# First layer norm: the inverse deviation over four columns, turned and spread by TensorE

## The chip, the cores and the metric

One core of a Trainium2 chip runs the whole computation in one launch. Its engines work side by side, each through its own queue in order, and meet by semaphores: TensorE (PE), VectorE (DVE), ScalarE (ACT), GpSimd (POOL), and SyncE (SP), which here only issues transfers. The metric is the device time of one execution in microseconds.

## The reference

The inputs are `x` (16 x 64 x 2048) and a context `ctx_4096` (16 x 1601 x 2048). Three blocks add to `x` in turn, each behind a layer norm:

```python
x = x + _L0_xattn_ref(_layernorm(x, axis=-1), ctx_4096, conv_w, bn_gamma, bn_beta)
x = x + _L0_attn_ref(_layernorm(x, axis=-1), wq, wk, wv, wo)
x = x + _L0_ffn_ref(_layernorm(x, axis=-1), gate_w, base_w, base_b, lora_A, lora_B)

def _layernorm(x, axis=-1, eps=1e-05):
    m = jnp.mean(x, axis=axis, keepdims=True)
    v = jnp.var(x, axis=axis, keepdims=True)
    return (x - m) / jnp.sqrt(v + eps)
```

The first block ranks, for each of the 16 batches and 2048 positions, the 1601 rows of the context, marks which of the 64 channels of `x` belong to the 38 highest of all, takes maximum and mean over the marked and the other channels, runs a short convolution with batch norm and sigmoid over them, and weights the channels. The second is causal attention with rotary positions (32 heads, 8 of keys and values), the third a linear layer with eight low-rank experts of which two are chosen.

The change is in the first layer norm: for each of the 16 x 64 = 1024 rows of `x` (a batch and a channel) a mean, a variance and 1 / sqrt(variance + eps) over 2048 positions.

## The kernel before, in words

**Layout.** `x` lies in SBUF as `XN`, 128 partitions x 2 halves x 16 steps x 512 columns. A column is one of the 1024 rows of `x` (8 batches x 64 channels a half), and its 2048 positions lie over 128 partitions x 16 steps. So a sum over positions is a product of a 128x128 matrix of ones with each of the 16 steps, added up in PSUM: each partition of the result then holds the same 512 sums. The mean and the inverse deviation of a half are therefore 128 x 512 tiles in which all 128 partitions are equal.

**The search around it.** The first 680 us rank the context. 256 tiles of 128 x 1601 values (16 batches x 16 steps) stream through a ring of 14 buffers; SP issues tile n when tile n - 14 has been used (`search_sync`, L426). A round `i` handles four tiles, in 66 rounds. DVE takes the eight largest of the 64 channels of each (L580) and bounds from them (L585), and writes, for each tile, two masks of what is larger than a bound, `b` and `c` (L440, one buffer of three after the other). ACT counts what is above another bound with a sign activation and its accumulator (`sign_scalar`, L642). PE adds up each mask, 13 products (`count_tensor`, L693), and ACT sums the result into a count (`counts_scalar`, L650). The counts decide the bounds of the next masks (L593, L601, L613, L617). POOL copies the 64 channels aside (L681).

**The layer norm inside it.** Its instructions are put into the queues between those of the search, at fixed rounds, by `LN0_SUM`, `LN0_MEAN`, `LN0_SUB` and `LN0_VAR`, each with a round for half 0 and one for half 1. In `search_vector` `ln0_vector` comes behind the fifth mask of a round (`k == 4`); in `search_scalar` `ln0_scalar` comes behind the fourth sign and the count of slot 1; in `search_tensor` `ln0_tensor` is called with `u` = 0 behind the second mask, with `u` = 1 behind the fourth, and so on. PE sums `XN` (L549), ACT scales to the mean (L531), DVE subtracts it in pairs of steps, every second round (L514), ACT squares one step a round into `lsq` (L539), and PE sums the squares (L556). Squares of half 1 run in rounds 41 to 56, so while half 0 gets its deviation in rounds 43 and 44. For half 0 (PSUM bank `ps[7]`, result tile `Rs`) and half 1 (`ps[6]`, result tile `Mn`) the deviation is made over the full 128 x 512: DVE multiplies by 1/L and adds eps (L520), ACT takes the root (L542), and a round later DVE the reciprocal (L523). When all masks are issued (`masked` reaches NMASKS) POOL multiplies `XN` by the result (`ln0_out_gpsimd`, L710), and the later stages begin.

## Time and profile before

| | us |
|---|---|
| median of 3 runs | 2283.42 |
| the three runs | 2282.82, 2283.42, 2288.04 |
| profiled execution | 2279.7 |
| its span | 2277.9 |
| DVE busy | 1402.7 (62%) |
| PE busy | 2004.4 (88%) |
| ACT busy | 1013.3 (44%) |
| POOL busy | 1021.4 (45%) |

The span is the time between the first and the last record of the profiled execution; its own time has some 1.8 us around it. The shares are means over stages with different limits: the search takes the first 680 us, then come the rest of the first block and, from about 860 us on, the products of attention and of the linear layer, in which PE is full. A row with a line number names the line of the kernel; where two numbers follow an arrow in brackets, the engine stood idle so long before the instruction, and what is named released it. Two records of one engine can overlap by some 0.1 us, so what an instruction costs its queue is read from its start to the start of the next one.

### The profile page before, as it was taken

The numbers are of one execution on the slowest core, as the hardware profiler recorded it, in microseconds if no ns is written. First come the engines' busy times: TensorE is split into PE (matmuls) and PEld (weight loads), VectorE is DVE, ScalarE is ACT, GpSimd is POOL, SyncE is SP. The second block draws the span as 40 slices with busy tenths as digits, with TensorE's granted clock in tenths as the row PEclk, the third lists the DMA queues.
The fourth block names the chain that finished last, engine by engine and source line by source line (L and its number), as shares of the span: only waits on it lengthen the run. The fifth ranks groups of instructions, "written<-read, shape, count | busy, mean of one in ns | idle before, by whom it ended". The sixth has DMA issues, their size and how long they took to land. (4 is left out here: it accounts for less than half of the span.)

```text
span 2277.9 us, 39061 instructions
## 1 busy us (share of the span) xinstructions
PE 2004.4 (88%) x15226; PEld 1633.7 (72%) x15226; DVE 1402.7 (62%) x2179; ACT 1013.3 (44%) x2014; POOL 1021.4 (45%) x930
## 2 busy tenths in 40 slices
PE   4778788777764947999999999999999999999999
PEld 3666566555554836787877888878778878888887
DVE  6999999999999989844444531144445425731111
ACT  7778788877840355423222422223223322422221
POOL 1223332222226522755564456556555445644554
PEclk9999999999987869999999999999999999999999
DMA  9999999889930114632225443322244345434443
GB/s 382 375 355 378 337 323 322 318 293 319 333 145 15 75 43 132 185 107 75 80 97 181 139 145 109 94 83 77 83 161 144 126 136 213 131 129 125 140 139 117
DMA packets 158392, 407.69 MB, mean 179 GB/s; under 512 B 15616, under 2 KB 44544, under 8 KB 156544
## 3 DMA queue, kind: packets, MB, share of 16 engines
q1 hardware_dynamic: 157920, 403.55, 51.7%
q8 instruction: 121, 1.98, 0.3%
q0 software_dynamic: 288, 1.64, 0.2%
q14 instruction: 63, 0.52, 0.1%
HBM read 379.96 MB, written 25.17 MB: 178 GB/s over the span
## 5 line engine op out<-in xcount | busy, mean ns | idle before, releaser
L1238 POOL TENSOR_TENSOR t<-t,t 128x512 fp32r<-128x512 f32 (+1 forms) x488 | 652.5, 1348 | 658.7 <-ACT t L1231 585.5
L1789 PE MATMUL ps<-t,t 128*128 128x512 f32 x1856 | 737.6, 397 | 12.4 <-POOL t L1238 7.1
L1791 PE MATMUL ps<-t,t 128*128 128x512 f32 x1856 | 723.8, 390 | 0.0
L1790 PE MATMUL ps<-t,t 128*128 128x512 f32 x1856 | 723.1, 390 | 0.0
L693 PE MATMUL ps<-t,t 128*128 128x128 bf16 (+1 forms) x6656 | 450.1, 221 | 181.3 <-DVE t L440 163.3
L1231 ACT ACTIVATE t<-t 128x512 fp32r<-128x512 f32 (+1 forms) x488 | 296.2, 608 | 696.1 <-PE ps L1791 381.6
L693 PEld LDWEIGHTS ps<-t,t 128*128 128x128 bf16 x6656 | 386.4, 100 | 279.8 <-DVE t L440 248.0
L440 DVE TENSOR_SCALAR t<-t,t 128x1601 bf16<-128x1601 f32 x512 | 516.2, 1050 | 4.6 <-DVE t L601 0.9
L642 ACT ACTIVATE t<-t,t 128x1601 bf16<-128x1601 f32 x256 | 416.9, 1628 | 62.7 <-DVE t L585 59.0
L1789 PEld LDWEIGHTS ps<-t,t 128*128 128x128 f32 x1856 | 348.3, 188 | 92.7 <-POOL t L1238 11.6
L1791 PEld LDWEIGHTS ps<-t,t 128*128 128x128 f32 x1856 | 348.3, 188 | 74.1
L1790 PEld LDWEIGHTS ps<-t,t 128*128 128x128 f32 x1856 | 348.7, 188 | 71.1 <-issue 1.4
L681 POOL COPY t<-t 128x64 f32<-128x64 f32 x256 | 163.2, 638 | 376.2 <-DMA t<-ctxT 375.9
L1749 DVE TENSOR_TENSOR t<-ps,t 128x512 f32<-128x512 f32 x32 | 22.1, 689 | 232.9 <-PE ps L1791 232.8
L1324 DVE SCALAR_TENSOR_TENSOR t<-ps,t 128x512 f32<-128x512 f32 x32 | 22.1, 691 | 177.0 <-PE ps L1316 177.0
L1746 DVE TENSOR_TENSOR t<-ps,t 128x512 f32<-128x512 f32 x32 | 22.1, 691 | 169.6 <-PE ps L1791 169.6
L650 ACT ACTIVATE t<-ps 128x128 bf16<-128x128 f32 x260 | 68.5, 263 | 92.8 <-PE ps L693 92.4
L1480 DVE TENSOR_REDUCE t<-t 128x128 f32<-128x2048 f32 x24 | 91.7, 3856 | 12.4 <-ACT t L1508 9.7
L1338 ACT ACTIVATE t<-t 128x512 f32<-128x512 f32 x32 | 20.2, 632 | 152.0 <-DVE t L1328 152.0
L562 PE MATMUL ps<-t,t 128*128 128x128 f32 x256 | 56.8, 398 | 29.7 <-POOL t L710 29.7
L562 PEld LDWEIGHTS ps<-t,t 128*128 128x128 f32 x256 | 53.5, 228 | 32.9 <-POOL t L710 30.3
L1271 POOL TENSOR_TENSOR t<-t,t 128x512 f32<-128x512 f32 x40 | 52.6, 1314 | 37.3 <-DVE t L1262 37.1
(210 smaller groups left out, 1692.9 us busy)
## 6 DMA issues: line engine op xcount, KB each, us to landing
t<-ctxT SPq DMA_DIRECT2D x256, 800.5 KB, 6.4
t<-wqkv SPq DMA_DIRECT2D x192, 256.0 KB, 3.1
t<-wo SPq DMA_DIRECT2D x128, 256.0 KB, 4.5
t<-wb SPq DMA_DIRECT2D x128, 256.0 KB, 3.5
t<-xT SPq DMA_DIRECT2D x48, 256.0 KB, 6.7
t<-x1d SPq DMA_DIRECT2D x32, 256.0 KB, 4.8
x2d<-t SPq DMA_DIRECT2D x32, 256.0 KB, 2.0
t<-x2d SPq DMA_DIRECT2D x8, 1024.0 KB, 7.4
```

The costliest lines, as they stand in the source:

```text
L440: e.tensor_scalar(Mb[k % 3][:, :], ring[n % NR][:, :], bound, None, ALU.is_gt).then_inc(masked, 1)
L562: return e.matmul(dst, ident, src, start=(c == 0), stop=(c == C - 1))
L642: e.activation(scr[:, :], ring[n % NR][:, :], ACT.Sign, bias=nT[:, n:n + 1], scale=SHRINK, accum_out=cntA[:, n:n + 1]).then_inc(signed, 1)
L650: e.activation(jr[:, :], ps[k % 6][:, 0:128], ACT.Copy, accum_out=sums[:, k:k + 1]).then_inc(counts_out, 1)
L681: e.tensor_copy(cand[b % 2][:, t, :], ring[n % NR][:, 0:C]).then_inc(cand_copied, 1)
L693: m = e.matmul(ps[s % 6][:, 0:w], (identh if kind == "b" else identb)[:, :], Mb[k % 3][:, 128 * c:128 * c + w], start=(first and c == 0), ...
L1231: e.activation(wh[r][:, 0:nk, :], raw[r][:, 0:nk, :], ACT.Copy).then_inc(w_hi, 1)
L1238: e.tensor_tensor(wlo[r][:, 0:nk, :], raw[r][:, 0:nk, :], wh[r][:, 0:nk, :].bitcast(F32), ALU.subtract).then_inc(w_lo, 1)
L1480: e.tensor_reduce(R1[:, cs], over_t((x if step == "s" else sq)[:, :, cs]), AX.X, ALU.add).then_inc(l_sum, 1)
L1789: e.matmul(bank[:, :], wh[r][:, q, :], xl, start=(kt == 0), stop=False)
L1790: e.matmul(bank[:, :], wlo[r][:, q, :], xh, start=False, stop=False)
L1791: m = e.matmul(bank[:, :], wh[r][:, q, :], xh, start=False, stop=(c == NCH[p] - 1 and q == nk - 1))
```

## The change

The deviation is the same in all 128 partitions of a 128 x 512 tile. The new code works it out once per column of a 128 x 4 tile, where the 512 values of a half lie over 128 partitions x 4 columns, and takes these steps (h is the half, `LN0_VAR` is now 43 and 58):

- round LN0_VAR: ACT copies the sums of squares from PSUM to SBUF (L545, semaphore `ln0_flat`)
- the round behind it: PE multiplies each of the four 128-column blocks of this copy, as weights, with one column of the identity, which lays the 512 sums over partitions, in four columns of PSUM (L573, `ln0_turned`); DVE scales and adds eps on 128 x 4 (L521); ACT takes the root in place (L548)
- the next: DVE takes the reciprocal of 128 x 4 (L524); ACT makes four copies of the 128 x 128 identity, scaled by partition with one of the four columns (L552), which is a row of diagonal blocks
- the next: PE multiplies a matrix of ones with them (L577), which spreads the 512 values over all partitions, and ACT copies the result to SBUF (L555, `ln0_rstd`)

```diff
-    LN0_SUM, LN0_MEAN, LN0_SUB, LN0_VAR = (15, 30), (23, 39), (24, 40), (43, 59)
+    LN0_SUM, LN0_MEAN, LN0_SUB, LN0_VAR = (15, 30), (23, 39), (24, 40), (43, 58)
...
+    ln0_inv = [sc[:, 40 + 4 * h:44 + 4 * h] for h in range(2)]
...
     def ln0_vector(e, i):
...
-            if i == LN0_VAR[h]:
-                e.wait_ge(ln0_sqsum, 16 * h + 16)
-                if h:
-                    e.wait_ge(ln0_sub, 16)
-                e.tensor_scalar(ln0_rs[h][:, :], ln0_sums[h][:, :], 1.0 / L, EPS, ALU.mult, ALU.add).then_inc(ln0_var, 1)
             if i == LN0_VAR[h] + 1:
+                e.wait_ge(ln0_turned, 2 * h + 1)
+                e.tensor_scalar(ln0_inv[h], ln0_sums[h][:, 0:4], 1.0 / L, EPS, ALU.mult, ALU.add).then_inc(ln0_var, 1)
+            if i == LN0_VAR[h] + 2:
                 e.wait_ge(ln0_std, h + 1)
-                e.reciprocal(ln0_rs[h][:, :], ln0_rs[h][:, :]).then_inc(ln0_rstd, 1)
+                e.reciprocal(ln0_inv[h], ln0_inv[h]).then_inc(ln0_var, 1)
 
     def ln0_scalar(e, i):
...
             if i == LN0_VAR[h]:
-                e.wait_ge(ln0_var, h + 1)
-                e.activation(ln0_rs[h][:, :], ln0_rs[h][:, :], ACT.Sqrt).then_inc(ln0_std, 1)
+                e.wait_ge(ln0_sqsum, 16 * h + 16)
+                if h:
+                    e.wait_ge(ln0_sub, 16)
+                e.activation(ln0_rs[h][:, :], ln0_sums[h][:, :], ACT.Copy).then_inc(ln0_flat, 1)
+            if i == LN0_VAR[h] + 1:
+                e.wait_ge(ln0_var, 2 * h + 1)
+                e.activation(ln0_inv[h], ln0_inv[h], ACT.Sqrt).then_inc(ln0_std, 1)
+            if i == LN0_VAR[h] + 2:
+                e.wait_ge(ln0_var, 2 * h + 2)
+                for c in range(4):
+                    e.activation(ln0_rs[h][:, 128 * c:128 * c + 128], ident, ACT.Copy, scale=ln0_inv[h][:, c:c + 1]).then_inc(ln0_flat, 1)
+            if i == LN0_VAR[h] + 3:
+                e.wait_ge(ln0_turned, 2 * h + 2)
+                e.activation(ln0_rs[h][:, :], ln0_sums[h][:, :], ACT.Copy).then_inc(ln0_rstd, 1)
 
     def ln0_tensor(e, i, u):
...
+            if i == LN0_VAR[h] + 1 and u == 0:
+                e.wait_ge(ln0_flat, 5 * h + 1)
+                for c in range(4):
+                    m = e.matmul(ln0_sums[h][:, c:c + 1], ln0_rs[h][:, 128 * c:128 * c + 128], ident[:, 0:1], start=True, stop=True)
+                m.then_inc(ln0_turned, 1)
+            if i == LN0_VAR[h] + 3 and u == 0:
+                e.wait_ge(ln0_flat, 5 * h + 5)
+                e.matmul(ln0_sums[h][:, :], ones, ln0_rs[h][:, :], start=True, stop=True).then_inc(ln0_turned, 1)
```

The new file is longer, so lines behind the edits have other numbers: the mask is L440 before and L441 now, the maxima L580 and L601, the sign activation L642 and L663, the counts L650 and L671 (ACT), the masks' products L693 and L714 (PE).

The order on ACT before, from the count of slot 1 in round 43 to the first sign of round 44 (t_131 is the result tile of half 0, t_78 the square, t_49 `XN`):

```order
L650 ACTIVATE t_79,t_143<-ps 128x128 [waits counts_out,counted]
L542 ACT_TABLE_LOAD
L542 ACTIVATE t_131<-t_131 128x512 [waits ln0_var]
L539 ACTIVATE t_78<-t_49 128x512 [waits ln0_sqsum,ln0_sub]
L650 ACTIVATE t_79,t_143<-ps 128x128 [waits counts_out,counted]
L642 ACTIVATE t_75,t_136<-t_66,t_133 128x1601 [waits signed,bound4]
```

And now, at the same place of round 43, of round 44 and of round 45 (t_150 holds the four columns, t_129 the constants with the identity):

```order
L545 ACTIVATE t_131<-ps 128x512 [waits ln0_sqsum]
L540 ACTIVATE t_78<-t_49 128x512 [waits ln0_sqsum,ln0_sub]
...
L671 ACTIVATE t_79,t_143<-ps 128x128 [waits counts_out,counted]
L548 ACT_TABLE_LOAD
L548 ACTIVATE t_150<-t_150 128x4 [waits ln0_var]
L540 ACTIVATE t_78<-t_49 128x512 [waits ln0_sqsum,ln0_sub]
...
L552 ACTIVATE t_131<-t_129,t_150 128x128 [waits ln0_var]
L552 ACTIVATE t_131<-t_129,t_150 128x128 x3
L540 ACTIVATE t_78<-t_49 128x512 [waits ln0_sqsum,ln0_sub]
```

The table load has moved from round 43 to round 44, and each of the three rounds has one group of work ahead of its square.

The order on PE before, behind the second mask of round 44 (t_72 and t_74 are mask buffers, t_139 and t_140 identities for the counts):

```order
L693 MATMUL ps<-t_74,t_140 128x65
L556 MATMUL ps<-t_78,t_129 128x512 [waits ln0_sq,ln0_mean]
L693 MATMUL ps<-t_72,t_139 128x128 [waits masked]
L693 MATMUL ps<-t_72,t_139 128x128 x11
L693 MATMUL ps<-t_72,t_139 128x65
```

And now:

```order
L714 MATMUL ps<-t_74,t_140 128x65
L573 MATMUL ps<-t_129,t_131 128x1 [waits ln0_flat]
L573 MATMUL ps<-t_129,t_131 128x1 x3
L569 MATMUL ps<-t_78,t_129 128x512 [waits ln0_sq,ln0_mean]
L714 MATMUL ps<-t_72,t_139 128x128 [waits masked]
```

The four products with one column stand between the second mask and the sum of the squares, so the third mask's count comes behind both.

The order on DVE before, around the reciprocal in round 44 (t_130 is the mean that L514 subtracts):

```order
L440 TENSOR_SCALAR t_74<-t_59,t_138 128x1601 [waits counted]
L523 RECIPROCAL t_131<-t_131 128x512 [waits ln0_std]
L514 TENSOR_TENSOR t_49<-t_49,t_130 128x1024 [waits ln0_mean]
L440 TENSOR_SCALAR t_72<-t_65,t_138 128x1601 [waits counted]
L440 TENSOR_SCALAR t_73<-t_60,t_138 128x1601 [waits counted]
```

And now, there and at the same place of round 45:

```order
L441 TENSOR_SCALAR t_74<-t_59,t_138 128x1601 [waits counted]
L521 TENSOR_SCALAR t_150<-ps 128x4 [waits ln0_turned]
L517 TENSOR_TENSOR t_49<-t_49,t_130 128x1024 [waits ln0_mean]
L441 TENSOR_SCALAR t_72<-t_65,t_138 128x1601 [waits counted]
...
L441 TENSOR_SCALAR t_73<-t_63,t_138 128x1601 [waits counted]
L524 RECIPROCAL t_150<-t_150 128x4 [waits ln0_std]
L441 TENSOR_SCALAR t_74<-t_69,t_138 128x1601 [waits counted]
```

The reciprocal of 512 columns behind the fifth mask of round 44 is gone; a short instruction stands there, and another one a round later.

## Rows read from the trace of the kernel before

**Rows 1.** Windows: length, busy of PE, PEld, DVE, ACT, POOL, then clock, DMA share, GB/s.
```profile
228.00:440.00 212.00, 169.84 (x2219) 130.82 (x2217) 209.29 (x430) 171.00 (x351) 65.02 (x104) 1.00 0.92 325
462.90:468.20 5.30, 5.28 (x66) 5.19 (x66) 4.86 (x12) 2.73 (x7) 0.06 (x1) 0.68 0.65 222
```

**Rows 2.** Waits of DVE, 100 to 640 us: waiter <- waited for: us, times, longest.
```profile
DVE t L580 <- DMA t<-ctxT: 1.6, 3, 0.9
DVE t L613 <- ACT t L650: 1.3, 3, 0.5
```

**Rows 3.** Waits of the SP queue, 0 to 700 us.
```profile
SPq L426 <- DVE t L440: 510.8, 235, 12.8
```

**Rows 4.** Timeline of DVE from 446.5 us: start, length, instruction, [idle before <- releaser].
```profile
447.07 0.67 DVE L520 TENSOR_SCALAR t<-ps 128x512 f32<-128x512 f32 x1
447.67 2.97 DVE L440 TENSOR_SCALAR t<-t,t 128x1601 bf16<-128x1601 f32 x3
...
453.71 0.17 DVE L613 TENSOR_SCALAR t<-t 128x4 uint32<-128x4 f32 x1 [0.47 <-ACT t L650]
```

**Rows 5.** Timeline of DVE from 457 us, the reciprocal of half 0.
```profile
457.48 3.34 DVE L523 RECIPROCAL t<-t 128x512 f32<-128x512 f32 x1
460.74 1.16 DVE L514 TENSOR_TENSOR t<-t,t 128x1024 f32<-128x1024 f32 x1
```

**Rows 6.** Costs by form: line, engine, shapes, count, busy us, mean ns, idle before.
```profile
L523 DVE RECIPROCAL t<-t 128x512 f32<-128x512 f32 x2 | 6.7, 3345 | 0.0
...
L520 DVE TENSOR_SCALAR t<-ps 128x512 f32<-128x512 f32 x2 | 1.4, 676 | 0.0
...
L1604 DVE RECIPROCAL t<-t 128x4 f32<-128x4 f32 x2 | 0.4, 178 | 0.1
...
L968 DVE TENSOR_SCALAR t<-ps 128x2 f32<-128x2 f32 x1 | 0.2, 159 | 0.7 <-PE ps L990 0.7
```

**Rows 7.** Timeline of DVE from 464 us, the round after the reciprocal.
```profile
467.73 0.17 DVE L613 TENSOR_SCALAR t<-t 128x4 uint32<-128x4 f32 x1 [0.33 <-ACT t L650]
...
469.12 0.34 DVE L580 MAX8 t<-t 128x8 f32<-128x64 f32 x2
```

**Rows 8.** Timeline of ACT from 445 us, the table load and the square root.
```profile
449.12 1.28 ACT L542 ACT_TABLE_LOAD   x1
450.41 0.63 ACT L542 ACTIVATE t<-t 128x512 f32<-128x512 f32 x1
450.95 0.61 ACT L539 ACTIVATE t<-t 128x512 f32<-128x512 f32 x1
...
451.72 1.62 ACT L642 ACTIVATE t<-t,t 128x1601 bf16<-128x1601 f32 x1
```

**Rows 9.** Costs by form of ACT, nearest to the added instructions.
```profile
L531 ACT ACTIVATE t<-ps 128x512 f32<-128x512 f32 x2 | 1.2, 587 | 0.0
...
L1007 ACT ACTIVATE t<-t,t,t 128x256 f32<-128x256 f32 x2 | 1.1, 584 | 0.0
...
L403 ACT ACTIVATE t<-t 128x128 fp32r<-128x128 f32 x1 | 0.3, 309 | 3.6 <-DMA t<-gw 3.6
...
L1003 ACT ACTIVATE t<-t 128x2 f32<-128x2 f32 x1 | 0.2, 203 | 10.6 <-DVE t L975 10.6
```

**Rows 10.** Costs by form of PE and of its weight loads, nearest to the added products.
```profile
L556 PE MATMUL ps<-t,t 128*128 128x512 f32 x64 | 35.3, 634 | 0.0
...
L562 PEld LDWEIGHTS ps<-t,t 128*128 128x128 f32 x256 | 53.5, 228 | 32.9 <-POOL t L710 30.3
...
L990 PEld LDWEIGHTS ps<-t,t 128*128 128x128 f32 x2 | 0.5, 310 | 10.9 <-DVE t L966 10.9
```

**Rows 11.** Timeline of POOL from 459 us, copies that follow a landed tile.
```profile
460.46 0.24 POOL L681 COPY t<-t 128x64 f32<-128x64 f32 x1 [2.63 <-DMA t<-ctxT]
```

**Rows 12.** Timeline of POOL from 640 us, first use of the inverse deviation.
```profile
681.23 18.46 POOL L710 TENSOR_TENSOR t<-t,t 128x1024 f32<-128x1024 f32 x8 [11.89 <-DVE t L440]
```

**Rows 13.** Timeline of DVE from 660 us, the end of the search.
```profile
676.78 0.17 DVE L613 TENSOR_SCALAR t<-t 128x4 uint32<-128x4 f32 x1 [2.22 <-ACT t L650]
```

More of the change, by code:

```diff
@@ L378, in build @@
     ln0_total, ln0_mean, ln0_sub, ln0_sq = sem("ln0_total"), sem("ln0_mean"), sem("ln0_sub"), sem("ln0_sq")
+    ln0_flat, ln0_turned = sem("ln0_flat"), sem("ln0_turned")
     ln0_sqsum, ln0_var, ln0_std, ln0_rstd, ln0_out = (sem("ln0_sqsum"), sem("ln0_var"), sem("ln0_std"),
```

## The prediction

> **What bounds the kernel now.** The change sits in the search, the first 680 us, so I read that stretch and not the shares of the whole span. The windows come first: from 228 to 440 us VectorE (DVE) is busy 209.29 of 212.00 us, PE 169.84, ACT 171.00, and the DMA engines 0.92 of the time at 325 GB/s [rows 1]. DVE is full and two others are not far behind, so the waits decide. Between 100 and 640 us DVE waited 1.6 us for a tile of the context and 1.3 us for ACT [rows 2]; the SP queue, which issues the tiles, waited 510.8 us for DVE's mask instruction L440 [rows 3]. The transfers are paced by DVE, not DVE by them. So a microsecond taken from DVE's queue here is a microsecond of the search, as long as ACT, PE and the tiles keep up. It is also one of the whole: the next stage begins when DVE has issued its last mask (POOL's L710 starts at 681.23, released by L440 [rows 12]), and what follows hangs on that point.
>
> **What DVE loses.** Half 0: L520 starts at 447.07 and the next mask at 447.67, so it holds the queue for 0.60 us [rows 4]. The reciprocal starts at 457.48, its successor at 460.74: 3.26 us [rows 5]. That is 3.86 us. Half 1 has instructions of the same length (means 676 and 3345 ns over both [rows 6]), so 2 x 3.86 = 7.72 us.
>
> **What DVE gains.** Per half a multiply-add over 4 columns out of PSUM and a reciprocal over 4 columns. The nearest rows are 159 ns (L968, 2 columns from PSUM) and 178 ns (L1604, 4 columns) [rows 6]. L520 lasted 0.676 and held the queue 0.60, the reciprocal 3.345 and 3.26: some 0.08 us of an instruction lies beside the next. Low end 2 x (0.159 + 0.178 - 0.16) = 0.36 us, high end without overlap 0.67. I take 0.4, near the low end, since both removed rows overlapped.
>
> **Waits that go.** Two of DVE's waits for ACT follow from what is removed. In round 43 ACT loads the table of the square root (449.12) and takes the root over 512 columns, and only at 450.95 goes on to its square [rows 8]: 1.83 us extra, after which DVE stands 0.47 us at L613 for the counts [rows 4]. After the change round 43 has only a copy from PSUM there, 587 ns by L531 [rows 9]. The other: during the reciprocal no masks come, PE stands idle, and from 462.90 to 468.20 its granted clock is 0.68 of full, a mixture of its two levels 1.2 and 2.4 GHz [rows 1]; PE is slow with the counts and DVE stands 0.33 us at L613 [rows 7]. With no pause this goes too. Together 0.80 us; low end 0, if something else is late at the same places.
>
> **What is added on ACT.** The first wait gives a measure of ACT's room: 1.83 us extra cost DVE 0.47, so 1.36 us beside the square is free in a round without a subtraction; an even round with the 1.16 us subtraction L514 on DVE [rows 5] has about 2.4. Round 44 (even): the table load, 1.28 us [rows 8], and a root over 4 columns, 0.203 by L1003 [rows 9], less overlap 0.1: 1.4 of 2.4. Round 45 (odd): four scaled copies of the 128x128 identity. The nearest plain copy is L403, 309 ns; L1007 with a scale and a bias in SBUF and twice the columns took 584 [rows 9]. Less 0.09 of overlap that is 0.22 to 0.49 each, 0.9 to 2.0 for four. I take 0.3 each, 1.2 in all, nearer to L403 since that has the shape: inside 1.36, with little to spare. At the high end DVE waits 2.0 - 1.36 = 0.6 us. Round 46: a copy of 0.59, inside. In half 1 the rounds 58 to 61 have no squares any more (the last is in round 56) and there is no second table load (the order of the changed kernel has one, before L548), so ACT has another half microsecond of room in each.
> The Trainium skill ("ScalarE: Activation LUTs", What ACT_TABLE_LOAD costs) says that each per-partition pointer operand adds about 93 ns to an ACTIVATE of 186 ns + 0.833 ns a column. By it a scaled copy is 386 ns and four with their overlap are an estimated 1.17 us, against 0.88 by L403 alone. It speaks against the change, since it takes up most of round 45's room; by the one as by the other DVE doesn't wait there, and the sum stays.
>
> **What is added on PE.** Round 44: four f32 products with a 128x128 weight load and one column each; a product shows as two records, so 8 loads, at 228 ns (L562) to 310 ns (L990) [rows 10]: 1.8 to 2.5 us, ahead of the column sum of the squares that is there already. Round 46: one product over 512 columns, 2 x 634 ns by L556's records [rows 10], some 1.1 to 1.3 us. PE is idle 42.16 of 212.00 us [rows 1]; 256 tiles in some 650 us make rounds of about 10.2 us, so about 2.0 us of each. DVE writes masks into three buffers and is about two masks (2 us) ahead of needing one back. 1.8 us fits; 2.5 us is over by 0.5, which would make ACT late with its counts or DVE wait for a buffer. Rounds 59 and 61 have no sums of squares and so more room. New waits in all: 0 to 0.5 + 0.6 = 1.1 us, and I take 0.3, since the loads cost most likely as L562's, which are in a stream, and not as the lone L990.
>
> **Who waits behind the new waits.** Behind DVE's wait for the turned sums (round 44, fifth mask) stand the subtraction and three masks; its releaser is on PE after the second mask of the same round, three masks (3 us) earlier in DVE's time, so it is done even with 2.5 us of products. ACT's root waits for that DVE instruction and comes after the fourth sign of the round, where ACT already came 2 us later than DVE's L520 (449.12 against 447.07 [rows 4, 8]). DVE's reciprocal waits for the root, a round old. PE's product in round 46 waits for the copies of round 45, which stand ahead of two counts and a sign.
>
> **Tiles.** A faster DVE frees ring buffers sooner. A tile landed at or before 460.46 [rows 11], and DVE first read it in the pair at 469.12 [rows 7]: 8.7 us ahead, and DVE moves up by 3.3 us only, with the issue of later tiles moved up by the same. No new wait.
> ln0_rstd becomes ready a round or two later than now, in round 46 and 61, but its first reader is L710 after the last mask [rows 12]: free.
>
> **Sum.** -7.72 + 0.4 - 0.80 + 0.3 = -7.8 us. The profiled execution (2279.7 us, span 2277.9) would become 2271.9. The median of before is 2283.42, 3.7 above it, and the same step from there gives 2275.6. By the ends of the terms: 7.72 - 0.67 - 1.1 = 5.95 us (2277.5) to 7.72 - 0.36 + 0.80 = 8.16 us (2275.3).
>
> **Rivals.**
> *ACT and PE keep some of it.* If round 44 or 45 comes out over its room in both halves, or ACT's lateness is handed on for a round, some 3 us come back: 2278.4. For it speaks that DVE stood 0.33 us in the round after the reciprocal with nothing extra on ACT [rows 7]; against it that ACT waits for DVE's bounds in the same round and so starts each one afresh.
> *The DMA engines become the bound.* They are 0.92 busy [rows 1]. If they can't follow, the saved 7.8 us turn into waits for tiles: about 2283. Against it: 1.6 us of such waits in 540 us [rows 2], the 8.7 us of lead, and a long-run pace that the change leaves as it is but for two short stretches.
> *The hand-overs land on DVE (slower).* The new chain goes ACT, PE, DVE, ACT, DVE, ACT, PE, ACT over four rounds. If the releaser came behind the waiter in each of rounds 44 to 46 and 59 to 61, DVE would stand as it does at the drained end of the search, 2.22 us [rows 13], six times: 13.3 - 8.1 (the gain without new waits) = +5.2, 2288.6. It decides from 8.1 / 6 = 1.35 us a round. Against it: every releaser stands at least two masks ahead in DVE's time.
>
> **Chances.** Forecast 0.65, the first rival 0.20, DMA 0.07, hand-overs 0.05, the rest for something else. A measurement of this kernel can tell about 0.3%, 6.85 us, from no change, so the border is at 2276.6, only 1.0 us above my number. Of the forecast's 0.65 I put 0.54 below it, since its own range 2275.3 to 2277.5 crosses it and the three runs of before differ by 5 us; with a little of the rest, faster 0.56, same 0.40, slower 0.04. The range: 2275.3 less 2 us for the spread of a median, 2273, up to the first rival with the same allowance, 2280.
>
> **What would show it.** Right: no DVE record of 3.3 us in the search, the search's last mask near 673.3 instead of 681.1; granted clock near 1.00 after the two places; L521's and L524's successors (by the new numbering) not preceded by idle time. PE's step would be wrong if the four one-column products took over 2 us, ACT's if the four scaled copies took over 1.36. The prediction is wrong as a whole if DVE shows new waits for ACT or for tiles of more than 2 us in all between 440 and 660 us, or if the end of the search moves up and the end of the kernel doesn't.

## The result, and the profile after

| | before | after |
|---|---|---|
| median of the runs compared, us | 2285.23 (12 runs) | 2275.94 (12 runs, 2272.05 to 2280.21) |
| profiled execution, us | 2279.7 | 2272.05 |
| its span, us | 2277.9 | 2270.2 |

One of the twelve runs of before took 3285.11 us, a thousand more than any other; it is a slow run, the ratio is taken without it, and the median of the other eleven is 2284.97.

The ratio of the times is 0.9967, with an interval of 0.9959 to 0.9974: 7.5 us faster, between 5.9 and 9.4. The medians lie 9.3 us apart, at the upper end of that. The forecast was 7.8 us and 2275.6.

The queue of DVE comes first. Here is half 0 in rounds 43 to 45, in the timeline (start, length, instruction, and idle time before it where there was any), at the place of [rows 4, 5, 7]:

```profile
452.15 0.16 DVE L634 TENSOR_SCALAR t<-t 128x4 uint32<-128x4 f32 x1
...
455.99 0.15 DVE L521 TENSOR_SCALAR t<-ps 128x4 f32<-128x4 f32 x1
456.06 1.21 DVE L517 TENSOR_TENSOR t<-t,t 128x1024 f32<-128x1024 f32 x1
457.20 2.97 DVE L441 TENSOR_SCALAR t<-t,t 128x1601 bf16<-128x1601 f32 x3
...
462.75 0.15 DVE L634 TENSOR_SCALAR t<-t 128x4 uint32<-128x4 f32 x1
...
466.52 0.17 DVE L524 RECIPROCAL t<-t 128x4 f32<-128x4 f32 x1
466.61 2.95 DVE L441 TENSOR_SCALAR t<-t,t 128x1601 bf16<-128x1601 f32 x3
```

No record of DVE above 2.5 us is left in the search. From the start of L521 to that of L517 it is 0.07 us, from L524's to the mask's 0.09, and no idle time stands ahead of either, nor ahead of L634, which is L613 of before, at the two places where it had stood 0.47 and 0.33 us [rows 4, 7].

The windows, first the undisturbed stretch, then the two places where PE used to run out of masks or just had (columns as in [rows 1]):

```profile
228.00:440.00 212.00, 169.85 (x2215) 130.79 (x2215) 209.30 (x430) 170.87 (x351) 62.48 (x103) 1.00 0.92 325
461.50:467.00 5.50, 4.60 (x60) 3.60 (x61) 5.39 (x12) 5.04 (x11) 1.54 (x3) 1.00 0.91 331
616.00:622.00 6.00, 4.57 (x72) 3.85 (x70) 5.97 (x10) 5.56 (x13) 2.59 (x4) 1.00 0.94 321
```

The first row repeats that of before to 0.03 us of PE and 0.01 of DVE, so the bound of the search is as it was. The granted clock is 1.00 (the 2.4 GHz level) behind both places, where it had been 0.68 behind the first [rows 1].

The waits of DVE from 100 to 640 us, which answer to [rows 2]:

```profile
DVE t L441 <- PE ps L714: 1.4, 1, 1.4
DVE t L441 <- DVE t L622: 0.8, 3, 0.3
```

None is for ACT and none for a tile. The 1.4 us for PE lie ahead of 250 us, far from the change, and the others are hand-overs of DVE to itself, 0.3 us each. The wait of the SP queue for the mask, 510.8 us before [rows 3], is now:

```profile
SPq L427 <- DVE t L441: 503.1, 236, 12.8
```

The transfers are still paced by DVE: with the search 9 us shorter, SP waits 7.7 us less, and DVE waits for no tile.

What was added, in the costs by form (count, busy us, mean ns), which answer to [rows 6, 9, 10]:

```profile
L524 DVE RECIPROCAL t<-t 128x4 f32<-128x4 f32 x2 | 0.3, 168 | 0.0
L521 DVE TENSOR_SCALAR t<-ps 128x4 f32<-128x4 f32 x2 | 0.3, 147 | 0.0
...
L552 ACT ACTIVATE t<-t,t 128x128 f32<-128x128 f32 x8 | 2.5, 393 | 0.0
L548 ACT ACT_TABLE_LOAD x1 | 1.3, 1283 | 0.0
...
L573 PEld LDWEIGHTS ps<-t,t 128*128 128x128 f32 x16 | 1.9, 192 | 0.0
```

And at their places in the timelines of ACT and of PE:

```profile
458.00 1.28 ACT L548 ACT_TABLE_LOAD   x1
459.29 0.20 ACT L548 ACTIVATE t<-t 128x4 f32<-128x4 f32 x1
...
468.45 1.27 ACT L552 ACTIVATE t<-t,t 128x128 f32<-128x128 f32 x4
```

```profile
453.01 1.03 PE L573 MATMUL ps<-t,t 128*128 128x1 f32 x8
453.90 1.10 PE L569 MATMUL ps<-t,t 128*128 128x512 f32 x2
```

Four scaled copies take 1.27 us in all, the eight records of the four turning products 1.03: a row with a count gives the length from the first start to the last end. From the first start to that of the next instruction it is 0.89 us for the products.

The end of the search, on POOL, and DVE's longest wait of its drain, which answer to [rows 12, 13]:

```profile
672.24 18.45 POOL L731 TENSOR_TENSOR t<-t,t 128x1024 f32<-128x1024 f32 x8 [11.35 <-DVE t L441]
```

```profile
667.79 0.17 DVE L634 TENSOR_SCALAR t<-t 128x4 uint32<-128x4 f32 x1 [1.69 <-ACT t L671]
```

POOL starts at 672.24 instead of 681.23, 8.99 us earlier, and the span is 7.7 us shorter.

### The profile page after: what moved, and what is told of

Its sections match the earlier page's. It is cut to its first block and busy times, and to the rows that moved or that the text cites. A ratio compares the mean times of both kernels' runs of the same rounds, so it can differ in the third digit from the quotient of the medians.

```text
span 2270.2 us, 39113 instructions
## 1 busy us (share of the span) xinstructions
PE 2004.8 (88%) x15246; PEld 1632.7 (72%) x15246; DVE 1392.3 (61%) x2179; ACT 1017.6 (45%) x2026; POOL 1022.7 (45%) x930
## 5 line engine op out<-in xcount | busy, mean ns | idle before, releaser
L714 PE MATMUL ps<-t,t 128*128 128x128 bf16 (+1 forms) x6656 | 447.6, 220 | 170.1 <-DVE t L441 151.7
L714 PEld LDWEIGHTS ps<-t,t 128*128 128x128 bf16 x6656 | 383.7, 99 | 269.4 <-DVE t L441 236.6
L441 DVE TENSOR_SCALAR t<-t,t 128x1601 bf16<-128x1601 f32 x512 | 516.5, 1051 | 5.9 <-PE ps L714 1.7
L663 ACT ACTIVATE t<-t,t 128x1601 bf16<-128x1601 f32 x256 | 416.9, 1628 | 61.8 <-DVE t L606 57.4
L671 ACT ACTIVATE t<-ps 128x128 bf16<-128x128 f32 x260 | 68.7, 264 | 80.0 <-PE ps L714 79.5
```

The lines of the kernel that those rows point to most:

```text
L441: e.tensor_scalar(Mb[k % 3][:, :], ring[n % NR][:, :], bound, None, ALU.is_gt).then_inc(masked, 1)
L663: e.activation(scr[:, :], ring[n % NR][:, :], ACT.Sign, bias=nT[:, n:n + 1], scale=SHRINK, accum_out=cntA[:, n:n + 1]).then_inc(signed, 1)
L671: e.activation(jr[:, :], ps[k % 6][:, 0:128], ACT.Copy, accum_out=sums[:, k:k + 1]).then_inc(counts_out, 1)
L714: m = e.matmul(ps[s % 6][:, 0:w], (identh if kind == "b" else identb)[:, :], Mb[k % 3][:, 128 * c:128 * c + w], start=(first and c == 0), ...
```

## Where the time came from

Each round of the search ends on DVE with one instruction that writes back a bound (L617 before, L638 after). Its start in the kernels of the experiments below, less its start in the first profile of before, shows in which rounds time was lost or won. The last two columns are differences of these shifts: half 0 is round 47 less round 43, half 1 is round 62 less round 59.

| kernel | 43 | 45 | 47 | 59 | 62 | 65 | half 0 | half 1 |
|---|---|---|---|---|---|---|---|---|
| before, start (us) | 443.42 | 467.93 | 489.50 | 611.28 | 643.06 | 676.98 | | |
| after | -0.50 | -4.99 | -4.85 | -5.00 | -8.61 | -8.99 | -4.35 | -3.61 |
| after_again | +0.82 | -3.79 | -3.52 | -3.55 | -7.20 | -7.88 | -4.34 | -3.65 |
| before_again | +1.92 | +2.29 | +2.37 | +2.48 | +3.26 | +3.08 | +0.45 | +0.78 |
| half1_only | +0.08 | +0.07 | +0.15 | -0.06 | -3.41 | -3.35 | +0.07 | -3.35 |
| recip_back | -0.33 | -1.01 | -0.84 | -1.01 | -0.73 | -1.58 | -0.51 | +0.28 |
| recip_split | +1.96 | +0.42 | +0.67 | +0.70 | +0.37 | +0.03 | -1.29 | -0.33 |
| early_table | +0.33 | +0.19 | +0.22 | -0.09 | +0.66 | -0.57 | -0.11 | +0.75 |
| copies_x2 | +2.48 | -2.09 | -0.67 | -0.90 | -3.07 | -3.37 | -3.15 | -2.17 |
| turn_x2 | -0.27 | -4.53 | -4.31 | -4.31 | -7.90 | -8.64 | -4.04 | -3.59 |
| turn_x3 | +2.89 | +0.70 | +0.83 | +0.82 | -2.70 | -3.10 | -2.06 | -3.52 |

Of the 8.99 us by which the first profile of after ends its search earlier, 4.35 + 3.61 = 7.96 lie in the two places of the change. 0.50 were there before round 43, 0.15 come between the halves and 0.38 in the drain; before_again stands 1.9 us off at round 43 with the same code, so differences of this size come without any change of the code. The experiments are read by the last two columns.

## The experiments

**The same two kernels again.** They show how far one profile can be trusted.

> The kernel before once more, for a second profile of it. Does it show the same two waits of DVE (0.47 us in round 44, 0.33 in round 45), or did they fall out differently, as in early_table, where the first was gone and the second had grown to 0.7, and half 1 had one of 0.7 that the first profile of before has not? If the room of ACT is a fixed 1.36 us, the 0.47 comes again to within 0.1; the wait behind the reciprocal may be anything from 0 to 0.7 in either half, as it follows PE's clock.

> The changed kernel once more, for a second profile. Expected: no wait of DVE for ACT between 430 and 640 us, and from round 43 to 47 and from 59 to 62 the same lengths as in its first profile to within 0.2 us, so that against before_again the two places give 7.2 (no waits in before) to 8.6 us (waits of 0.47, 0.7 and 0.7).

Measured: before 2282.70 us (span 2280.9), after 2276.39 (2274.6). The changed kernel repeats its two local gains to 0.04 us. The kernel before doesn't repeat its times: it lost another 0.45 and 0.78 us at the two places. These are its waits of DVE from 430 to 640 us, and two windows behind the reciprocals:

```profile
DVE t L613 <- ACT t L650: 1.8, 3, 0.7
DVE t L440 <- DVE t L601: 0.6, 2, 0.3
```

```profile
464.00:470.00 6.00, 5.13 (x54) 5.14 (x54) 5.30 (x10) 2.25 (x7) 0.44 (x1) 0.53 0.55 190
630.00:637.00 7.00, 5.46 (x54) 5.46 (x55) 6.25 (x13) 2.57 (x7) 0.85 (x1) 0.51 0.64 228
```

The single waits are 0.47, 0.68 and 0.68 us, 1.8 in all where the first profile had 0.80. PE's granted clock was 0.53 and 0.51, which is nearly all of the stretch at the lower level.

What sets the wait behind the pause can be read in the records. Before DVE's L613 can run, ACT must take the count of the second mask that PE adds up behind the pause (L650), then a sign and the next count; where DVE waits, L613 starts 2.27 us behind that first count. These are the first counts in the first profile of before (half 0, half 1) and in before_again (half 0), with the windows of PE's clock around them:

```profile
465.46 0.28 ACT L650 ACTIVATE t<-ps 128x128 bf16<-128x128 f32 x1 [5.42 <-PE ps L693]
...
631.08 0.28 ACT L650 ACTIVATE t<-ps 128x128 bf16<-128x128 f32 x1 [4.26 <-PE ps L693]
```

```profile
467.75 0.28 ACT L650 ACTIVATE t<-ps 128x128 bf16<-128x128 f32 x1 [5.77 <-PE ps L693]
```

```profile
462.90:463.30 0.40, 0.38 (x7) 0.38 (x8) 0.40 (x1) 0.00 (x0) 0.06 (x1) 1.00 0.00 0
463.40:466.70 3.30, 3.30 (x36) 3.29 (x34) 3.26 (x9) 1.24 (x3) 0.00 (x0) 0.50 0.57 180
```

```profile
464.90:469.60 4.70, 4.70 (x47) 4.70 (x48) 4.40 (x9) 1.85 (x4) 0.44 (x1) 0.50 0.59 197
```

This is every pause behind one long reciprocal in the profiles (times in us; the runs are those told of below):

| place | PE starts again | its clock falls to the lower level | second mask done | DVE waits for the counts |
|---|---|---|---|---|
| before, half 1 | 629.06 | 1.54 later | 1.99 later | no |
| half1_only, half 0 | 463.02 | 0.52 later | 2.48 later | 0.31 |
| before, half 0 | 462.93 | 0.42 later | 2.50 later | 0.33 |
| before_again, both halves | 464.87, 631.54 | is low already | 2.85 later | 0.68 |
| early_table, both halves | 462.77, 629.01 | is low already | 2.85 later | 0.68 |
| recip_back, both halves | 461.56, 618.31 | is low already | 2.85 later | 0.69, 0.68 |

So the wait follows from how much of the first two masks behind the pause PE adds up at the lower level, and how long PE stays there afterwards makes no difference: the low stretch that began in the pause lasts about twice as long in before_again as in recip_back, with the same wait. Why the clock falls at one moment or the other in the same program is open.

The removed waits are worth 0.8 to 1.8 us, then; against before_again the changed kernel wins 4.35 + 0.45 + 3.61 + 0.78 = 9.2 us in the two places, more than the 8.6 expected as the most.

**Half 1 alone.** Half 0 keeps the old code on all engines.

```diff
+            if h == 0 and i == LN0_VAR[0]:
+                e.wait_ge(ln0_sqsum, 16)
+                e.tensor_scalar(Rs[:, :], ps[7][:, :], 1.0 / L, EPS, ALU.mult, ALU.add).then_inc(ln0_var, 1)
+            if h == 0 and i == LN0_VAR[0] + 1:
+                e.wait_ge(ln0_std, 1)
+                e.reciprocal(Rs[:, :], Rs[:, :]).then_inc(ln0_rstd, 1)
...
-            if i == LN0_VAR[h] + 1:
-                e.wait_ge(ln0_turned, 2 * h + 1)
+            if h and i == LN0_VAR[h] + 1:
+                e.wait_ge(ln0_turned, 1)
...
```

> Half 0 makes its deviation as before (512 columns on DVE in rounds 43 and 44), half 1 as in the changed kernel. Theory A (DVE's queue: what leaves it is saved, and nothing else counts): half 1 alone saves 3.86 us of removed instructions less 0.2 of added ones, 3.5 to 3.7 us between the round starts 59 and 62, and rounds 42 to 47 are as before; the kernel lands near 2281.5 by the medians, ratio to the kernel before 0.9984. Theory B (what is saved is the wait behind the table load and behind PE's lost clock, which half 1 does not show as a wait): half 1 alone saves under 1 us, ratio 0.9996 or more. If the halves don't add up, the change's own 7.8 us in the two places would differ from the sum of 4.3 and 3.5.

Measured: 2279.21 us, ratio 0.9980 (0.9972 to 0.9989), 4.6 us faster. By rounds it gains nothing in half 0 and 3.35 in half 1. The waits of half 0 stand again as before:

```profile
453.80 0.17 DVE L643 TENSOR_SCALAR t<-t 128x4 uint32<-128x4 f32 x1 [0.47 <-ACT t L680]
...
467.80 0.17 DVE L643 TENSOR_SCALAR t<-t 128x4 uint32<-128x4 f32 x1 [0.31 <-ACT t L680]
```

The 0.47 is equal to the hundredth to that of [rows 4] and of before_again: it isn't chance; early_table below shows that it goes with the table load. The parts add up to 0.3 us: 3.35 here, where the whole change has 3.61 in half 1 (3.5 to 3.7 were expected), and the other 4.35 only where half 0 is changed too. Of the missing 0.26 us a new wait for ACT in round 60 has 0.18.

**The long reciprocal back beside the new chain.** A reciprocal over the flat 512 sums, whose result the copies then overwrite, is put in front of L521; everything else of the change stays. DVE's L521 stands behind it, so ACT's root waits for it too, and so do ACT's scaled copies a round later.

```diff
             if i == LN0_VAR[h] + 1:
                 e.wait_ge(ln0_turned, 2 * h + 1)
+                e.reciprocal(ln0_rs[h][:, :], ln0_rs[h][:, :]).then_inc(warm, 1)
...
```

> The changed kernel with one more instruction a half: a DVE reciprocal over 128x512, in place on the tile that PE has just turned (it is overwritten later, so its result is not used), at the old place behind the fifth mask of rounds 44 and 59. Theory A (DVE's queue time): 2 x 3.26 = 6.5 us of the gain go again, the kernel ends within 1 us of 0.9994 of before (2282 to 2283.5), and PE again stands idle about 4.5 us at both places with the granted clock near 0.7 behind it. Theory B (table load and clock): the table load is still in round 44 and hidden, so only the waits through PE's clock, 0.3 to 1 us, come back, and it stays near 2276.

Measured: 2282.93 us, ratio 0.9999 (0.9990 to 1.0008): nothing is left of the gain. By rounds it costs 3.84 and 3.89 us against after. That is more than the 3.26 of queue time, and the timeline shows the rest:

```profile
456.04 3.35 DVE L521 RECIPROCAL t<-t 128x512 f32<-128x512 f32 x1
459.30 0.10 DVE L522 TENSOR_SCALAR t<-ps 128x4 f32<-128x4 f32 x1
...
466.71 0.17 DVE L636 TENSOR_SCALAR t<-t 128x4 uint32<-128x4 f32 x1 [0.69 <-ACT t L673]
```

The counts come 0.69 us late behind the pause. This is PE there, and the two windows:

```profile
454.93 2.27 PE L716 MATMUL ps<-t,t 128*128 128x128 bf16 x39
461.56 5.40 PE L716 MATMUL ps<-t,t 128*128 128x128 bf16 x65 [4.36 <-DVE t L441]
```

```profile
461.50:467.00 5.50, 5.35 (x66) 5.07 (x67) 4.75 (x12) 2.55 (x7) 0.09 (x1) 0.74 0.65 186
616.00:622.00 6.00, 3.69 (x42) 3.68 (x43) 5.96 (x12) 1.01 (x4) 1.27 (x2) 0.72 0.53 190
```

PE had nothing to do for 4.36 us and then ran its 65 products of five masks in 5.40 us, at a granted clock of 0.74. Half 1 shows the same wait, 0.68. So a long instruction of DVE costs here the 3.26 us that it holds the queue and 0 to 0.7 us more behind it, and one instruction accounts for nearly the whole difference of the two kernels (3.84 of 4.35 us, and 3.89 of 3.61).

**The same work in four pieces.** The reciprocal over 512 columns is cut in four of 128, each ahead of one of the masks 5 to 8 of the round. It asks whether the wait behind the pause comes from PE, with its pause and its clock, or from the work that the change adds on ACT.

```diff
+    def ln0_pieces(e, i, k):
+        for h in range(2):
+            if i == LN0_VAR[h] + 1 and k >= 4:
...
+                q = slice(128 * (k - 4), 128 * (k - 3))
+                e.reciprocal(ln0_rs[h][:, q], ln0_rs[h][:, q]).then_inc(warm, 1)
...
```

> As recip_back (an added DVE reciprocal over the 512 columns of each half, its result not used), but cut into four of 128 columns, behind the fifth to eighth mask of rounds 44 and 59, so that DVE's time is the same and a little more (4 x 0.82 to 0.9 us) and PE is never without masks for over 2 us. Theory A1 (the waits of 0.69 and 0.68 us for ACT behind the whole reciprocal come from PE, which idles 4.4 us, loses its clock to 0.74 and counts late): the granted clock stays at 0.95 or more in the 5.5 us behind, the waits at that place are 0.1 us or none, and each half costs 3.3 to 3.6 us against the changed kernel instead of 3.8 and 3.9. Theory A2 (the waits come from ACT's own added work): they stay at 0.6 to 0.7 us.

Measured: 2284.14 us, ratio 0.9992 (0.9982 to 1.0002). By rounds it costs 3.06 and 3.28 us against after, 0.8 and 0.6 less than in one piece and somewhat under the 3.3 to 3.6 expected. It is also less than the 3.45 us for which the four pieces hold the queue (0.86 each from start to start); In half 0 DVE's hand-over to itself in round 46, 0.28 us, is absent here; the rest is open. These are the pieces and the two windows:

```profile
L532 DVE RECIPROCAL t<-t 128x128 f32<-128x128 f32 x8 | 7.5, 937 | 0.0
```

```profile
461.50:467.00 5.50, 3.82 (x39) 3.25 (x39) 5.46 (x11) 2.11 (x6) 0.47 (x2) 0.69 0.64 221
616.00:622.00 6.00, 3.43 (x48) 2.93 (x46) 6.00 (x10) 2.13 (x7) 0.47 (x2) 0.83 0.87 284
```

DVE's longest wait for ACT from 430 to 640 us is 0.2 us, with all of ACT's added work in place, so that work isn't the cause. But PE's clock is only 0.69 and 0.83 there, where 0.95 or more was expected. A low clock alone doesn't make DVE wait, then. At the lower level PE takes 1.33 us a mask from start to start (before_again, behind 464.87); behind the whole reciprocal DVE gives it a mask every 0.97 us, here one every 1.74 with a piece beside each, and PE keeps up. The prediction gave the second wait to the clock alone, and that is half of it.

**The table load moved out of the search.** On the kernel before, a root over four columns at the very start loads the table, and the root in round 43 needs no load.

```diff
+        e.activation(sc[:, 60:64], cst[:, 0:4], ACT.Sqrt)
```

> The kernel before with a square root over four columns in ACT's setup, so that the table is there from the start and no load stands in round 43. If the 0.47 us wait of DVE in round 44 came from the load and the root together (1.83 us against a room of 1.36), it is gone here, since the root alone is 0.54: round 45 starts 0.4 to 0.5 us earlier against round 43 than in the kernel before. If it came from something else (the last mask of round 43 being late behind L520), it stays. The reciprocal's wait of 0.33 us in round 45 stays in both.

Measured: 2280.47 us in one run, span 2278.7. The 0.47 us at L613 are gone: round 44 comes 0.56 us earlier against round 43. A round later DVE waits 0.68 us instead of the 0.33 of [rows 7]:

```profile
467.92 0.17 DVE L614 TENSOR_SCALAR t<-t 128x4 uint32<-128x4 f32 x1 [0.68 <-ACT t L651]
```

So half 0 as a whole gains only 0.11 on the first profile of before. The longer wait doesn't come from the moved load: before_again has the same 0.68 with the load in its old place, and against it half 0 gains 0.11 + 0.45 = 0.56 us. In the changed kernel both waits go, the first because the load stands in round 44, where it costs none, the second because the long instruction goes. In half 1 this run loses 0.75, as before_again does with 0.78: the 0.68 us behind the second reciprocal is there in some executions of before and not in others.

**Twice the scaled copies.** Four more of the same shape go to PSUM and are overwritten. This asks for ACT's room.

```diff
                 for c in range(4):
+                    e.activation(ln0_sums[h][:, 128 * c:128 * c + 128], ident, ACT.Copy, scale=ln0_inv[h][:, c:c + 1]).then_inc(ln0_flat, 1)
+                for c in range(4):
...
```

> The changed kernel with each of the four scaled identity copies made twice, the first time into PSUM columns that are overwritten a round later. They took 1.27 us for four, so ACT has 1.2 us more in rounds 45 and 60. By the room of 1.36 us beside the square (half 0) and some 1.9 us without it (half 1), DVE should wait about 2.45 - 1.36 = 1.1 us in round 46 and 2.45 - 1.9 = 0.55 us in round 61. If ACT's room is in truth much larger (theory: ACT is only 0.8 busy, so a second microsecond is free), no wait shows.

Measured: 2281.29 us in one run, span 2279.5. By rounds it costs 1.20 and 1.44 us against after. These are the waits, first that of half 0, then the larger of half 1:

```profile
476.45 0.17 DVE L636 TENSOR_SCALAR t<-t 128x4 uint32<-128x4 f32 x1 [1.15 <-ACT t L673]
...
630.41 0.17 DVE L636 TENSOR_SCALAR t<-t 128x4 uint32<-128x4 f32 x1 [0.89 <-ACT t L673]
```

The 1.36 us of room that the prediction read out of the first wait held for half 0: 1.1 us were expected and 1.15 came. In half 1, where it gave ACT half a microsecond more, 1.2 us came in two waits instead of 0.55; there is hardly more room than in half 0. The four copies of the change fit by some 0.1 us.

**Twice and three times the turning products.** This asks for PE's room in round 44 and 59.

```diff
-                for c in range(4):
+                for c in range(8):
+                    c = c % 4
```

> The changed kernel with the four one-column products made twice: 16 loads, about 1.95 us instead of 1.03, which is what the prediction took for the eight (1.8 to 2.5). In turn_x3 another 1.8 us cost 2.29 us in round 44 and nothing in round 59. If PE had some room left in round 44 (here 0.9 us are added), the cost is 0 to 0.5 us; if it stands at its edge there, 0.9 to 1.2 us. In round 59 nothing. This says what the change would have lost, had the loads taken what was predicted.

> The changed kernel with the four one-column products made three times (the same results again). Four took 1.03 us on PE, so PE has 2.1 us more in rounds 44 and 59, beside 2.0 us that it is idle in a round. Expected: in round 44, where the sum of the squares stands behind them, PE is about 1.2 us late with the third mask, which shows as 0 to 1 us of waits of DVE for PE or ACT; in round 59 none. If PE's in-order queue were the tightest place, as the rival of a slow PE has it, DVE would wait 2 us in both.

Measured: 2274.05 and 2279.76 us in one run each, spans 2272.2 and 2278.0. The products of half 0 with twice, then with three times their number:

```profile
453.14 1.92 PE L574 MATMUL ps<-t,t 128*128 128x1 f32 x16
```

```profile
456.32 2.82 PE L574 MATMUL ps<-t,t 128*128 128x1 f32 x24
```

That is 1.03, 1.92 and 2.82 us for 8, 16 and 24 loads: 0.11 us each, where the prediction took 0.23. By rounds the cost against after in half 0 is 0.31 us for twice and 2.29 for three times; in half 1 it is 0.02 and 0.09. DVE's waits with three times the number, in half 0:

```profile
461.60 1.06 DVE L441 TENSOR_SCALAR t<-t,t 128x1601 bf16<-128x1601 f32 x1 [1.10 <-PE ps L715]
462.93 2.02 DVE L441 TENSOR_SCALAR t<-t,t 128x1601 bf16<-128x1601 f32 x2 [0.28 <-PE ps L715]
...
468.42 0.17 DVE L635 TENSOR_SCALAR t<-t 128x4 uint32<-128x4 f32 x1 [0.86 <-ACT t L672]
```

First no mask buffer is free, then the counts are late: 2.24 us, nearly all of the 2.29, and more than the 0 to 1 us expected. PE's room in round 44 ends just below 1.92 us, and 0.9 us over it costs not 0.9 but 2. Half 1, with no sums of squares, takes the 2.82 us at a cost of 0.09.

**The same kind of edit where PE is full.** The four long reciprocals of the later layer norms (after 680 us) are left out in effect: one runs over 4 columns, three are copies, so those inverses are not computed.

```diff
-        e.reciprocal(Rs[:, :], Rs[:, :]).then_inc(p_rstd, 1)
+        e.reciprocal(Rs[:, 0:4], Rs[:, 0:4]).then_inc(p_rstd, 1)
...
-            e.reciprocal(rs[:, :], R1[:, :]).then_inc(l_rstd, 1)
+            e.tensor_copy(rs[:, :], R1[:, :]).then_inc(l_rstd, 1)
```

> The changed kernel, in which the four later reciprocals over 128x512 (one in the second layer norm's tables at about 892 us, three from 1302 us on) are left out: the first is cut to 4 columns, the others are replaced by a copy, so what they compute is left out. It asks whether the same edit would pay there. If, as the windows say, PE is full from 900 us on (397 of 400 us), the three hidden ones are worth nothing, and the first, which DVE runs while PE still waits now and then, up to 3 us: 2273 to 2276. If the reciprocals were on the path everywhere it would be 4 x 3 = 12 us, 2264.

Measured: 2275.03 us, ratio 0.9965 (0.9954 to 0.9977), against 0.9967 with them. The copies still take 0.4 to 1.5 us each, so some 10 of the 13.4 us of records are gone. This is the window from 900 to 2200 us of this kernel, which holds the last three of the four (the first stands at 894 us):

```profile
900.00:2200.00 1300.00, 1287.82 (x7466) 1046.05 (x7466) 525.10 (x628) 395.34 (x664) 711.46 (x530) 1.00 0.39 125
```

PE is busy 1287.82 of 1300 us and DVE 525. Some 10 us less on DVE show as 0.0002 of the ratio, half a microsecond, where the interval is about 2.6 us to either side: not the instruction decides, but which engine is full around it.

**The subtraction given to POOL.** This tried to win more: L517, sixteen instructions of 1.23 us on DVE, moves to POOL, which is busy less than a third of the search [rows 1].

```diff
+    def ln0_gpsimd(e, i):
+        for h in range(2):
+            x, j = XN[:, h, :, :], (i - LN0_SUB[h]) // 2
+            if LN0_SUB[h] <= i < LN0_SUB[h] + 16 and (i - LN0_SUB[h]) % 2 == 0:
+                e.wait_ge(ln0_mean, h + 1)
+                e.tensor_tensor(x[:, 2 * j:2 * j + 2, :], x[:, 2 * j:2 * j + 2, :], bc(Mn[:, :], 2),
+                                ALU.subtract).then_inc(ln0_sub, 1)
...
```

> The changed kernel with the mean's subtraction (16 instructions of 128x1024, 1.08 us each of DVE's queue) moved from DVE to POOL, behind its fourth copy of the same rounds. Theory A says that DVE's queue is the bound, so up to 16 x 1.08 = 17.3 us go: 2259 to 2263 (ratio 0.990). It is less if ACT, which then has 1.1 us less room in each of those rounds, or PE is late: ACT's round with a square is about 9.7 us against DVE's 9.8 without the subtraction, so 5 us may stay. The rival: POOL's instruction, 2.3 us by its like in the stage behind the search, slows DVE's masks through the shared SBUF port (DVE's short instructions took 2.2 us instead of 0.3 beside POOL's there), and the kernel gets no faster, 2276 or more.

Measured: 2300.30 us, ratio 1.0072 (1.0057 to 1.0087), 16 us slower than before, where after is 7.5 us faster. The theory that DVE's queue alone decides was wrong here by some 40 us, and its rival right. These are DVE and POOL in the same microseconds:

```profile
315.25 3.21 DVE L441 TENSOR_SCALAR t<-t,t 128x1601 bf16<-128x1601 f32 x1
```

```profile
315.27 2.35 POOL L527 TENSOR_TENSOR t<-t,t 128x1024 f32<-128x1024 f32 x1
```

The mask takes 3.21 us where it takes 1.05 alone, longer by the 2.2 us in which POOL's subtraction runs. DVE pays 2.1 to 2.2 us a piece for the 1.1 it was relieved of, some 17 us over the sixteen, and the mean of the mask from 240 to 640 us rises from 1051 to 1166 ns. Another 7 us are waits: DVE's waits of that stretch grow from 0.8 us to 8.2, of which 6.0 are for ACT's counts. The Trainium skill ("GPSIMD Engine Reference", Specifications) has POOL share its SBUF interfaces with VectorE, with contention where VectorE runs in a 2-port mode or reads two SBUF inputs. The trace agrees that they contend: 1.05 and 2.35 us of work take 3.21 us side by side, so here the two exclude each other almost wholly. Which of the two conditions the mask meets no run here tells.

No version that computes the whole result is shown to be faster than the changed kernel; the one run of turn_x2, 2274.05 us, lies inside the spread of the changed kernel's own twelve.

## Why the prediction was right

*What bounds the search.* Right. DVE 209.30 of 212 us as before, no tile waited for, SP waiting 503.1 us for the mask. That 3.84 us come back with one instruction (recip_back) and none with four of them elsewhere (later_short) shows it.

*What DVE loses, 7.72 us.* Right: both records are gone, and recip_back gives 3.26 of the 3.86 back as queue time.

*What DVE gains, 0.4 us.* Measured were 2 x (0.07 + 0.09) = 0.32. The records last 147 and 168 ns, and about half of each lies beside its neighbour. My low end of 0.36 was still above it.

*Waits that go, 0.80 us.* Right in sum for the first profile, and both are gone in both profiles of after. Two things were wrong in it. The clock alone doesn't make the second wait (recip_split has the clock and not the wait). And it isn't a fixed quantity: by the moment at which the clock falls it is 0.33 in one half and nothing in the other, and 0.68 in both in the next execution. In the second profile of before the waits that go were 1.8 us. That the forecast took 0.80 was right for the one trace it was read from.

*Added on ACT.* Round 44 had 1.40 us (from 458.00 to the next start at 459.40) against 1.4, round 45 1.27 against 1.2. By the rule of the Trainium skill ("ScalarE: Activation LUTs", What ACT_TABLE_LOAD costs) a scaled copy was an estimated 386 ns; the trace has 393 and so agrees, and L403's 309 would have been too low. The room of 1.36 us is what copies_x2 confirms in half 0 and corrects in half 1.

*Added on PE.* This is the term that was mis-sized: 1.8 to 2.5 us forecast for the eight loads, 1.03 measured. A load with its one column starts 0.11 us behind the one before, though its record lasts 192 ns; I had multiplied records, and longer ones of other instructions, instead of distances between starts. The 0.3 us that I took as cost therefore didn't come: with 1.92 us, near my low end, turn_x2 pays 0.31. So the price was right for the length I believed in, and the length was not. The flat "2.0 us of idle time a round" was a fair place for the border and a poor guide to the price beyond it.

*Sum.* In the two places -7.72 + 0.32 and the waits of 0.80 give -8.2 for the first profile; the rounds show -7.96, the forecast was -7.8. It was nearer than its terms: the 0.3 us for PE didn't come, and 0.24 us of what the terms give don't show in the rounds, 0.15 of it in half 0 and 0.09 in half 1. What took them is open. That two misses nearly cancel is luck. So is the 2275.6: it was counted from the 2283.42 of three runs, and the median of before is now 2285.23, from which the same 7.8 us give 2277.4.

*The end of the search and of the kernel.* 672.24 was 1.1 us earlier than the 673.3 of the forecast. Of that 0.5 us stem from before the change and 0.4 from the drain, where the wait fell from 2.22 to 1.69. Of the 8.99 us 1.3 were given back after the search. The stretch behind it varies by several microseconds between executions: from round 65 to the end 1600.9 and 1600.8 us in the two profiles of before, 1602.2 and 1605.5 in the two of after, 1603.9 in turn_x2, 1602.0 in half1_only. At 1966 us of the first profile of after, PE waits 1.7 us for POOL; the second profile has this wait too (1.65), neither profile of before has it, and turn_x2 and turn_x3, with the same code there, don't have it either. Why is open; that the changed kernel loses 1 to 2 us there of what the search wins is possible by these numbers and not shown.

*The rivals.* DMA as the new bound: no wait for a tile, refuted. Hand-overs that land on DVE: L521 and L524 have no idle time ahead of them, refuted. ACT and PE keeping some: not in the change itself, but closer than it looks, since four more copies on ACT (1.17 us) or 0.9 us more on PE in half 0 already cost 1.20 and 0.31. (Three microseconds back from 2275.6 would be 2278.6, not the 2278.4 of the forecast.)

## What to carry to other kernels

Read the distance from one start to the next on the engine that is full, not the record; then ask what its long instructions starve, because a 3.3 us instruction on the engine that feeds the others cost 3.8 us here. A chain of small steps over other engines was cheap because each step was shorter than the idle time of its engine in that round and its waiter stood several instructions behind; measure that room by doubling the step. The same edit was worth nothing where another engine is full. And take a wait of a few tenths of a microsecond from more than one profile before you put it into a sum.

## What was not expected of the hardware

- Eight f32 weight loads of 128x128, each with a one-column product, took 1.03 us (16 took 1.92, 24 took 2.82), 0.11 us each from start to start at a granted clock of 1.00.
- A mask on DVE (f32 in, bf16 out, 1601 columns) and a subtraction of two SBUF operands on POOL (1024 columns) don't run side by side: 3.21 us instead of 1.05 beside POOL's 2.35 (pool_sub).
- After 4.36 us without work PE's granted clock was 0.74 over the next 5.5 us (recip_back), in before_again 0.53 and 0.51 over 6 to 7 us. The same program differs in the moment at which the clock falls, and so does the wait behind it: none where it fell 1.54 us after PE's new start, 0.33 where 0.42 after, 0.68 where before it.
- A reciprocal on DVE lasts 168 ns over 4 columns, 937 over 128 and 3345 over 512.
